# A selective scan re-tiled from 8 channels by 16 states to 32 channels by 4 states

## What is computed

```python
def step(h, inp):
    dtt, ut, bt, ct = inp
    dA = jnp.exp(dtt[..., None] * A)
    h = h * dA + (dtt * ut)[..., None] * bt[:, :, None, :]
    y = jnp.einsum('bkdn,bkn->bkd', h, ct)
    return (h, y)
```

## Time and profile before

| | us |
|---|---|
| median of 3 runs | 3044.75 |
| lowest, highest | 3038.03, 3046.68 |
| the profiled execution: its time | 3046.35 |
| its span, first to last instruction | 3044.2 |
| its mean granted PE clock | 0.832 of full speed |

### The profile page before, as it was taken

How to read it: one execution, slowest core, us unless ns; L and a number is a source line. 1 busy time by engine, 2 the same in 40 slices (tenths; PEclk the granted TensorE clock), 3 DMA queues, 4 the chain that set the end, 5 groups by cost and what they waited for, 6 DMA issues and landing times. The chain is left out here.

```text
span 3044.2 us, 33683 instructions
## 1 busy us (share of the span) xinstructions
PE 2434.6 (80%) x9156; PEld 870.9 (29%) x9156; DVE 2226.7 (73%) x3030; ACT 1408.0 (46%) x1949; POOL 1310.4 (43%) x677
## 2 busy tenths in 40 slices
PE   4776767676677676767667689999999969999999
PEld 2111111111111111111113312323233216676676
DVE  4899989999999998999965588878787843221122
ACT  3344444444444454444545416767676732212221
POOL 1678877878778887778772200000000020000000
PEclk9776767777777776777767869999999969999999
DMA  3455555555555555555541431312213160000000
GB/s 90 131 166 161 157 155 155 171 157 153 158 162 150 164 171 146 158 151 159 161 114 49 105 44 23 43 24 34 34 23 43 23 144 1 11 6 6 6 6 11
DMA packets 104457, 291.18 MB, mean 96 GB/s; under 512 B 15262, under 2 KB 21057, under 8 KB 104257
## 3 DMA queue, kind: packets, MB, share of 16 engines
q1 hardware_dynamic: 103194, 289.13, 36.5%
q10 hardware_dynamic: 1102, 0.19, 0.0%
HBM read 239.66 MB, written 25.88 MB: 87 GB/s over the span
## 5 line engine op out<-in xcount | busy, mean ns | idle before, releaser
L529 POOL TENSOR_TENSOR hs<-hs,bc 128x1024 f32<-128x1024 f32 x384 | 899.9, 2355 | 218.8 <-DVE hs L615 218.6
L502 ACT ACTIVATE decay<-decay,a_neg 128x1024 f32<-128x1024 f32 x384 | 440.6, 1148 | 670.4 <-DMA decay<-dt_rows 659.3
L426 PE MATMUL psU<-stack,spread_sel 96*128 96x512 bf16 x768 | 361.4, 488 | 437.4 <-DVE hs L615 341.8
L1447 DVE TENSOR_REDUCE mx<-ps 128x1 f32<-128x512 f32 x864 | 539.5, 684 | 115.3 <-PE ps L1286 110.2
L559 DVE TENSOR_TENSOR psU<-psU,bc 128x512 f32<-128x512 f32 x768 | 517.3, 677 | 27.1 <-issue 14.9
L1422 ACT ACTIVATE P<-ps 128x512 f32<-128x512 f32 x768 | 417.7, 599 | 247.1 <-PE ps L1298 222.9
L615 DVE TENSOR_TENSOR_SCAN hs<-decay,psU 128x512 f32<-128x512 f32 x384 | 466.2, 1214 | 77.3 <-PE psY L388 49.0
L615 DVE TENSOR_TENSOR_SCAN hs<-decay,hs,psU 128x512 f32<-128x512 f32 x384 | 488.9, 1273 | 1.1
L388 PE MATMUL psY<-hs,state_sel 128*32 128x512 f32 x1572 | 398.5, 849 | 23.7 <-DVE Y L572 11.1
L1286 PE MATMUL ps<-ks,qs 96*128 96x512 bf16 x864 | 344.3, 402 | 34.5 <-DMA ks<-qk_parts 23.8
L426 PEld LDWEIGHTS psU<-stack,spread_sel 96*128 96x128 bf16 x768 | 70.8, 100 | 1005.9 <-DVE hs L615 806.4
(11 more groups left out here) (239 smaller groups left out, 2381.2 us busy)
## 6 DMA issues: line engine op xcount, KB each, us to landing
decay<-dt_rows SPq DMA_DIRECT2D x388, 512.0 KB
stack<-parts SPq DMA_DIRECT2D x297, 64.0 KB, 5.6
dt_rows<-dt SPq DMA_DIRECT2D x33, 384.0 KB, 6.9
qs<-qk_parts SPq DMA_DIRECT2D x90, 128.0 KB, 6.7
ks<-qk_parts SPq DMA_DIRECT2D x90, 128.0 KB, 7.1
qk_parts<-qparts SPq DMA_DIRECT2D x16, 576.0 KB, 3.6
X<-in_x_dram SPq DMA_DIRECT2D x4, 768.0 KB, 9.9
raw<-in_x_dram SPq DMA_DIRECT2D x4, 768.0 KB, 10.5
```

The costliest lines, as they stand in the source:

```text
L426: pe.matmul(psU[:, q % UR, :], s.spread_sel[:, gg, :], stack[:, ui % 2, j, CH * pos:CH * pos + CH], start=True, stop=True).then_inc(dtu_sp ...
L502: nc.scalar.activation(decay[:, t % DR, :], decay[:, t % DR, :], ACT.Exp, scale=s.a_neg[:, col:col + 1]).then_inc(decay_ready, 1)
L529: pool.tensor_tensor(h, h, bc[:, 2 * p + r, 1, :], ALU.mult).then_inc(hc_ready, 1)
L1447: v.reduce_max(mx[:, slot, u:u + 1], ps1[:, (slot * MAXES + u) % R, :], AX.X).then_inc(max_done, 1)
```

## The change

A tile becomes 32 channels by 4 states: partition 32 q + d holds channel d of block j and state 4 q + nq. Tile t has nq = t // 3 and j = t % 3. So one replicated copy of dt of 32 channels (4 times over the partitions) serves the four tiles of a j, and is loaded three times a unit into `dt_rep`, beside dt times u into `dtu_rep` (4 buffers each). `decay` is now written from `dt_rep`, with a wait for the half scan eight back. C is stored to DRAM once per four units and loaded for each nq, four rows 32 times each, into `c_rep`. B is what PE spreads, in three bf16 parts from `b_stack`, and DVE multiplies it with `dtu_rep`. The projections of B and C for both directions of an order are one 64 row product at ui 2 and 6. dt is prepared one unit ahead, at the unit's start, in place of two ahead at its end. `hs` has 8 buffers and its waits come two tiles later. `prepare` loads the A logs by four DMAs in pieces of 4 numbers, gives its semaphores back and ends in a barrier. The diff, cut to its core:

```diff
...
+                for q in range(4):
+                    act.dma_start(a_exp[BLK * q:BLK * q + BLK, :].rearrange("p (g n) -> p g n", n=SUB),
+                                  w.alog.rearrange("(g d) (q n) -> q d g n", d=BLK, q=4)[q]).then_inc(a_in, 16)
                 act.dma_start(wdt_rows[:], w.wdt.rearrange("k (f p) r -> p (k f) r", p=HC)).then_inc(wdt_in, 16)
...
+        nc.clear_and_free_semaphores(sems)
+        nc.all_engine_barrier()
...
-        HR, DR, UR = 6, 4, 4
+        HR, DR, UR, RR = 8, 4, 4, 4
         xt = sb("xt", [HC, 2, L])
-        bc = sb("bc", [128, 4, 2, L])
         dt = sb("dt", [HC, L])
         soft = sb("soft", [HC, L])
-        dtu = sb("dtu", [HC, L])
-        rest = sb("rest", [HC, L])
-        parts = sb("parts", [HC, QPART, L], BF16)
-        stack = sb("stack", [HC, 2, NBLK, L], BF16)
+        rows = sb("rows_bc", [3 * 2 * N, L])
+        b_stack = sb("b_stack", [3 * 2 * N, 2, L], BF16)
+        c_rep = sb("c_rep", [128, SUB, L])
+        dt_rep = sb("dt_rep", [128, RR, L])
+        dtu_rep = sb("dtu_rep", [128, RR, L])
         decay = sb("decay", [128, DR, L])
         hs = sb("hs", [128, HR, L])
...
+        S0 = 2 * DR + START
...
+                    if q >= 4:
...
+                                pe.matmul(psU[:, q % UR, :], s.b_sel[:, r, nq, :],
+                                          b_stack[:, p, CH * pos:CH * pos + CH],
+                                          start=True, stop=True).then_inc(b_spread, 1)
+                                z_side(q, b, ui)
+                                row_side(q, b, ui, n)
...
+                    if t in (1, 2):
...
+                            nq, j = t // NBLK, t % NBLK
+                            col = (6 * k + 3 * f + j) * SUB + nq
+                            if nq == 0:
+                                act.wait_ge(dt_in[rep_slot(ui, j)], rep_count(b, ui, j))
+                            act.wait_ge(scan_done, n * (2 * TILES) + (2 * t + 2 - 2 * DR + S0))
+                            nc.scalar.activation(decay[:, t % DR, :], dt_rep[:, rep_slot(ui, j), :], ACT.Exp,
                                                  scale=s.a_neg[:, col:col + 1]).then_inc(decay_ready, 1)
-                            bc_side(t, b, ui, n)
-                            split_side(t, n + 1, b, ui)
-                            z_side(t, unit_ahead(b, ui)[1], n + 2)
-                            if ui == UNITS - 2 and t in (7, 8):
-                                h = t - 7
-
+                            z_side(t, unit_ahead(b, ui)[1], n + 1)
+                            row_side(t, b, ui)
...
+                            nq = t // NBLK
+                            if t % NBLK == 0:
+                                pool.wait_ge(c_in[nq], n * 16 + 16)
+                            pool.wait_ge(scan_done, n * (2 * TILES) + (2 * t + 2 + S0))
+                            h = hs[:, h_slot(ui, t), :]
+                            pool.tensor_tensor(h, h, c_rep[:, nq, :], ALU.mult).then_inc(hc_ready, 1)
+                            if t == 3:
+                                pool.wait_ge(log_ready, n + 2)
                                 pool.tensor_tensor(dt[:], dt[:], soft[:], ALU.add).then_inc(dt_ready, 1)
-                            if t == 11:
-                                pool.wait_ge(dt_ready, n + 3)
+                            if t == 4:
+                                pool.wait_ge(dt_ready, n + 2)
                                 if np_:
                                     pool.wait_ge(xt_half, nb * 2 + 2)
                                 pool.sem_inc(dtu_begun, 1)
-                                pool.tensor_tensor(dtu[:], dt[:], source(nb, np_)(nf, 0, L),
-                                                   ALU.mult).then_inc(dtu_ready, 1)
...
+                    if t < NBLK and q % 2 == 0:
+                        v.wait_ge(dtu_in[rep_slot(ui, j)], rep_count(b, ui, j))
...
+                    v.tensor_tensor(u, u, dtu_rep[:, rep_slot(ui, j), CH * pos:CH * pos + CH], ALU.mult
+                                    ).then_inc(dbu_ready, 1)
...
-                                v.wait_ge(summed, n * SUB + (SUB + q // 6 + START))
+                                v.wait_ge(summed, n * SUB + (SUB + q // 6))
+                            if q % 6 == 4:
+                                v.wait_ge(summed, n * SUB + (SUB + q // 6 + 1))
...
-                def store(par):
-                    sp.dma_start(s.dt_dram[par], dt[:]).then_inc(dt_stored, 16)
-
-                def stack_up(part, slot):
-                    for j in range(NBLK):
-                        sp.dma_start(stack[BLK * part:BLK * part + BLK, slot, j, :],
-                                     parts[BLK * j:BLK * j + BLK, part, :]).then_inc(stacked[slot], 16)
-
-                def load(par, t):
-                    d = rows_of(t)
-                    src = s.dt_dram[par, d:d + DD, :].unsqueeze(1).broadcast_to([DD, N, L])
-                    sp.dma_start(decay[:, t % DR, :], src).then_inc(landed[t % DR], 16)
-
+                def store(i, par, tile, done):
+                    sp.dma_start(s.dt_dram[par, i], tile[:]).then_inc(done, 16)
+
+                def spread_rows(i, par, rep, landed, ui, j):
+                    src = s.dt_dram[par, i, BLK * j:BLK * j + BLK, :].unsqueeze(0).broadcast_to([4, BLK, L])
+                    sp.dma_start(rep[:, rep_slot(ui, j), :], src).then_inc(landed[rep_slot(ui, j)], 16)
+
+                def load_dt(ui, j):
+                    spread_rows(0, ui % 2, dt_rep, dt_in, ui, j)
+
+                def load_dtu(ui, j):
+                    spread_rows(1, ui % 2, dtu_rep, dtu_in, ui, j)
+
+                def load_c(ui, nq):
+                    p, f, r, k = order(ui)
+                    src = s.c_dram[p].rearrange("(r q n) l -> r n q l", r=2, q=4)[r, nq]
+                    sp.dma_start(c_rep[:, nq, :], src.unsqueeze(1).broadcast_to([4, BLK, L])).then_inc(c_in[nq], 16)
+
+                def store_c(p):
+                    sp.dma_start(s.c_dram[p], rows[C_ROWS, :]).then_inc(c_stored, 16)
+
+                sp.wait_ge(row_taken, 2)
+                store_c(0)
                 sp.wait_ge(dt_ready, 1)
-                store(0)
+                store(0, 0, dt, dt_stored)
+                sp.wait_ge(dtu_ready, 1)
+                store(1, 0, soft, dtu_stored)
                 sp.wait_ge(dt_stored, 16)
-                for t in range(DR):
-                    load(0, t)
-                for part, ready in enumerate((hi_ready, mid_ready, lo_ready)):
-                    sp.wait_ge(ready, 1)
-                    stack_up(part, 0)
+                load_dt(0, 0)
+                sp.wait_ge(dtu_stored, 16)
+                load_dtu(0, 0)
+                for j in (1, 2):
+                    load_dt(0, j)
+                    load_dtu(0, j)
+                sp.wait_ge(c_stored, 16)
+                for nq in range(SUB):
+                    load_c(0, nq)
                 with sp.Fori(0, NB, 1) as b:
                     for ui in range(UNITS):
                         n = b * UNITS + ui
+                        nu = (ui + 1) % UNITS
+                        par = nu % 2
+
+                        def c_free(nq):
+                            sp.wait_ge(hc_ready, n * TILES + (3 * nq + 3 + TILES + START))
+
                         sp.wait_ge(dt_ready, n + 2)
-                        store((ui + 1) % 2)
-                        for t in range(TILES):
-                            if t == TILES - DR:
-                                sp.wait_ge(dt_stored, n * 16 + 32)
-                                sp.sem_inc(rows_kept, 1)
-                            sp.wait_ge(scan_done, n * (2 * TILES) + (2 * t + 2 + S0))
-                            if t + DR < TILES:
-                                load(ui % 2, t + DR)
-                            else:
-                                load((ui + 1) % 2, t + DR - TILES)
-                            if t in (4, 5, 7):
-                                part = (4, 5, 7).index(t)
-                                sp.wait_ge((hi_ready, mid_ready, lo_ready)[part], n + 2)
-                                stack_up(part, (ui + 1) % 2)
-                for i in range(DR):
-                    sp.wait_ge(landed[i], NB * UNITS * (16 * TILES // DR) + 16)
-                sp.wait_ge(stacked[0], (NB * UNITS // 2 + 1) * (16 * QPART * NBLK))
+                        store(0, par, dt, dt_stored)
+                        if nu in (0, 4):
+                            sp.wait_ge(c_stored, b * 32 + (32 if nu else 48))
+                            sp.sem_inc(turn_seen, 1)
+                        c_free(0)
+                        load_c(nu, 0)
+                        sp.wait_ge(dtu_ready, n + 2)
+                        store(1, par, soft, dtu_stored)
+                        sp.wait_ge(dt_stored, n * 16 + 32)
+                        sp.sem_inc(turn_seen, 1)
+                        sp.wait_ge(decay_ready, n * TILES + 1)
```

(48 more changed lines are left out.)

278 lines of the change are left out of this document (124 added, 154 removed).

## The result

The changed kernel takes **3678.43 us** (median of 4 runs, 3677.36 to 3680.35) against 3044.58 us for the kernel before on the same chip: a ratio of 1.2087, with a 95% interval of 1.2066 to 1.2108. The forecast was 4235 us with a range from 3690 to 4550. The direction came out as said, and so did the mechanism, loads that wait for four busy DMA engines; the size did not: the loss is 634 us in place of 1190, and the measured time lies 12 us under the lower end of the range.

A forecast was written before the change was run, and what follows sets the result against it. It took four full DMA engines to bound the changed kernel, eight before: 3046.4 - 1474 for the old loop + 2617 for 32 units of 81.8 + 46 at the ends = 4235 us; range 3690 to 4550.

The forecast's parts named there:

- the cut: Row loads of the scan: the source's slowest count, now 4, limits each to the same four DMA engines; chance 0.88.
- the cycle: Scan unit: 3u of loads, 13.4 us until SP stores dt, then the queue restarts; 81.8 us a unit.
- T: Scan unit: the moment j=0's dt*u rows have landed, which DVE's first product waits for.
- u: Scan: time of one 512 KB load on four engines at 18.4 GB/s each, 7.12 us.
- 9u + 17.7: Length of one scan unit, nine loads on its path plus fixed time: 81.8 us, 32 units 2617.
- 3655: Total in us at the bound of 25.5 GB/s an engine: u 5.14, unit 64.0.
- First product: Start of the scan: DVE's first product at 81, +5.5 us, counting 8 for wdt_rows and 2u for loads.
- 8u for 3u + 15: First scan unit: dt 1 and 2 and all C also queue, so it restarts at 8u; +21 us.
- Tail: Behind the last scan unit: loads for a next one still run, 4u where 8.9 us stood; +19.5 us.
- Eight engines: Rival for the scan's loads: they still go over eight engines, unit 49.7 us, total 3177; chance 0.05.
- Sixteen with DVE as the bound: Rival for the scan's loads: all sixteen engines serve them, DVE bounds, loop 1390, total 2957; chance 0.06.
- PE's wait: Unit's start without a DMA bound: PE late by 0 to 2.6 us, 0.4 taken; chance 0.01.

The follow-up runs named there:

- the two versions that undo it: Changed kernel with each load of a unit as four DMAs of 32 partitions: 2955.86 us; or with partitions numbered (channel, state), one DMA a load: 2944.61 us.
- The turned order: Changed kernel with C's first load ahead of SP's wait for dt, and dt's first load ahead of the wait for dt*u: 3644.50 us.
- 16x8: Phase of a kernel that only loads: 16 rows, each 8 times running, into 128 partitions; 237 GB/s.
- 8x16: Phase of a kernel that only loads: 8 rows, each 16 times running, into 128 partitions; 126 GB/s.
- 8x8: Phase of a kernel that only loads: 8 rows, each 8 times running; 127 GB/s.
- 4x32: Phase of a kernel that only loads: 4 rows, each 32 times running, into 128 partitions; 4x31 went the same.

## Why the prediction was right and wrong

**Right: the cut.** The forecast has it that "a transfer is cut over as many of the 16 DMA engines as that slowest count allows", and that the new loads "use four engines, the same four each time". Shares of 0.25 after, 0.13 with a count of 2, 0.26 in the kernel before with a count of 4, and up to 1.06 and 0.96 in the two versions that undo it show it in both kernels and in both directions. The rule of the Trainium skill ("DMA: Bandwidth & Descriptors", Rules for kernel authors), that a leading repetition of c copies confines a DMA to at most c engines, is borne out by these runs for 2, 4 and 8.

**Right: the cycle.** T + 3u + 13.4, then the queue anew. In the unit at 994.83, 3u took 15.23 us, from the third dt*u to the store of dt 13.6 passed (1010.06 to 1023.67), and from the store to the next T the unit before took 35.9 (958.98 to 994.83), where 6u + 4.3 give 34.8. In the mean of 31 units the three stretches are 15.3, 13.6 and 36.3. The formula 9u + 17.7 with the measured 5.08 is 63.4 for a mean of 65.2, and 1.5 of the 1.8 us between them lie in the third stretch. The turned order shortened that stretch and no other, by less than half of what was worked out.

**Wrong: u, the term in "7.12".** It measured 5.08, 26 GB/s an engine. "I take the loop's mean of 18.4, since it was measured on the same kind of load under the same engines' work" is the step that failed. The mean of eight engines on loads of 8 rows, 16 times each, says nothing of four on 32 rows a copy: alone, 8 rows 16 times each move 127 GB/s, 16 an engine, and the same eight engines do 26 with 15 repetitions in place of 16; four copies of 32 rows move 104, 26 an engine. The better row stood in the same group: 204 GB/s in one stretch, 25.5 an engine. That an engine can do this was seen directly, and a mean below it had to be explained before it was carried over. The Trainium skill ("DMA: Bandwidth & Descriptors", Specifications) gives some 27 GiB/s (29 GB/s) an engine, which by our estimate would have made u 4.5 us; the traces show 26.5 at most for such loads.

The term is large since it stands nine times in each of 32 units: 288 x (7.12 - 5.08) = 588 us too much. The unit's other terms measured 58 us more than the formula has (65.2 - 63.4, 32 times), which takes as much off again; the small terms below add 28, and so the 557 us come out by which the forecast was too high. The range was cut at 25.1 GB/s, just inside the upper bound of 25.5 that the text itself gave. A bound that was seen in a row belongs inside the range. (At the other end 16.3 leaves out the 125 GB/s of the same rows, 15.6 an engine.) And 3655, my sum for that bound, has 11 us too much in the terms ahead of the loop and behind it; with u = 5.14 in all of them it is 3644.

**The small terms.** First product: 81 said, 73.39 measured. The four loads of the A logs held `wdt_rows` back from 8.04 to 18.5 us, more than the 8 that I took, but the scan's block began at 38.3, only 1.0 later than before, since that chain had slack (PE first used these rows at 19.95 before and at 20.99 now): 7 us too much. The 2u in the term are 4.1 too much as well, and 3.5 us between block and product were missing. The first unit took 73.9, 8.7 over the others, where 8u for 3u + 15 gives 10.4. Tail: by the mean the queue's T would come again at 2103.3 + 65.2 = 2168.5, and 4u later is 2188.8; the next stage starts at 2189.24. So the loads of a unit that never comes are waited for, as said:

```profile
2189.24 2.48 POOL L823 TENSOR_TENSOR lc_both<-Y 96x512 f32<-96x512 f32 x2 [32.07 <-POOLq L349]
```

**The rivals.** Eight engines (3177) is excluded by the share. Sixteen with DVE as the bound (2957, with a loop of 1390) is what the two repaired versions are: 2955.9 and 2944.6, and a loop of 1379 in the second. PE's wait was priced at 0.4 us a unit and is 11.3/32 = 0.35 there. So the sum for everything else in this change was 11 us too high in the loop and within 13 in all, and had its loads been written with another outer dimension it would have gained 3.5%.

## What to carry to other kernels

Before counting the bytes of a DMA, look at the outermost dimension of its source and its destination: a repetition of 2, 4 or 8 put there left the other engines empty here, and a mean DMA share of 0.25 that didn't move with the work around it was four full engines and not slack. If data has to be repeated over partitions, choose the order of the partitions so that the long dimension is outermost (32 rows, each four times), and turn the masks instead; it cost nothing here and was at least as fast as four smaller DMAs. The rate of an engine on loads of one shape isn't its rate on another (13 to 26 GB/s here, all of them busy): keep every rate that the trace shows inside the range, and where the term stands nine times in a unit, time the new shape alone.

## What was not expected of the hardware

An engine's rate goes with how a load is cut more than with whether its rows repeat. With a count of 8, 8 rows 16 times each and 128 different rows both went at some 127 GB/s; with a count of 16, 16 rows 8 times each and 128 different rows both at some 237. On the same eight engines 15 repetitions in place of 16 made 207, and on the same sixteen 32 rows 4 times in one DMA made 385 to 402. What is read isn't quite without effect: one row for all 128 partitions went at 274 to 318, 128 different ones at 394 to 423. No run tells the source's part in this from the destination's.

DMAs of 32 or 64 partitions stayed near 240 GB/s with all engines at a share of 1.0, where one of 128 reaches 394 to 423. The Trainium skill ("SBUF — State Buffer", Door 1: The DMA port swizzle) has a map by which 32 or 64 partitions in a row reach only 8 of 16 ports, and 64 are no faster than 32. The runs agree with the second, and with half of the full rate roughly (0.6 of 400 measured). If the engines of one DMA kept step, that map would by our estimate give 16x8 eight ports at a time and 8x16 and 8x8 four, which fits the order of their rates (237, 126, 127). It would give 4x32 two, and that form ran at 26 GB/s an engine, so this reading is not shown.

A split load that alone takes 2.2 us cost about 4 in the mean when it took turns with loads that fill four of the engines (36 us for eight loads).

It stays open why the kernel before has two levels, 125 and 204 GB/s at the same share, with loads of one shape; no run was made for that.
